# One kernel, one change: more head sums on TensorE, layer normalisation moved to the head of the step, scatters split over two steps

## The reference

```python
x = x + attn(xn) + ffn(xn)
# attn: 8 heads of 16 within each row; no row looks at another
q, k, v = split(xn @ W_qkv.T + b_qkv); each head of q, k, v is divided by its norm
q, k     -> three rounds of mixing neighbouring heads (entangle)
scores   = |einsum('sid,sjd->sij', conj(q), k)|**2 * gain[c]       # 4 circuits c
w        = sqrt(softmax(scores, -1) + 1e-12)
weighted = einsum('sij,sjd->sid', w, v)                            # 4 circuits
out      = sum over c of sup[c] * sign(weighted) * clip(|weighted|, 1e-6, 1), times a phase, @ W_out.T + b_out
# ffn: top-2 of 8 experts per row, gelu(x @ W1[e] + b1[e]) @ W2[e] + b2[e], weighted by a softmax of two
```

## Time and profile before

| | us |
|---|---|
| median of 3 runs | 1745.51 (1744.3 to 1752.1) |
| the profiled execution | 1748.88 |
| its span, first to last instruction | 1747.1 |
| busy: VectorE, TensorE, GpSimd, ScalarE | 1376.4, 1228.0, 889.0, 772.2 |
| mean granted clock of TensorE | 0.837 of 2.4 GHz |

### The profile page before, as it was taken

One profiled execution on the slowest core, in us unless ns is written; L12 is line 12 of the kernel. 1 busy time (PEld: TensorE's weight loads), 2 busy tenths in 40 slices (PEclk: granted clock), 3 DMA queues, 4 the chain that ended last, 5 costly groups with the idle time before them and its releaser, 6 DMA issues.

```text
span 1747.1 us, 19553 instructions
## 1 busy us (share of the span) xinstructions
PE 1228.0 (70%) x6013; PEld 939.7 (54%) x6013; DVE 1376.4 (79%) x1622; ACT 772.2 (44%) x1606; POOL 889.0 (51%) x579
## 2 busy tenths in 40 slices
PE   4576878676787887677877777778677777876221
PEld 2354756555475665555556465656456565655121
DVE  5548888877888888987888898976879798888763
ACT  4344544345454454535435463644345354442110
POOL 1343515476353645477355363667536363536674
PEclk9988988788898888888878898889788898887565
DMA  7242322224223231433314232333213232230101
GB/s 225 69 128 82 91 74 68 84 70 120 70 87 88 69 108 49 122 97 94 91 37 126 62 115 67 93 97 103 87 49 116 67 109 74 87 89 18 31 14 46
DMA packets 110669, 147.24 MB, mean 84 GB/s; under 512 B 14921, under 2 KB 84198, under 8 KB 110054
## 3 DMA queue, kind: packets, MB, share of 16 engines
q1 hardware_dynamic: 101350, 125.01, 23.9%
q0 software_dynamic: 8192, 16.79, 3.1%
q10 hardware_dynamic: 1024, 4.20, 1.9%
HBM read 113.81 MB, written 32.13 MB: 84 GB/s over the span
## 4 chain that ended last, share of the span: by engine, by line
PE 36%; DVE 25%; POOL 15%; issue 15%; ACT 7%; DMA 1%; SPq 0%; ACTq 0%; POOLq 0%; DVEq 0%
POOL prod L1212 11%; PE ps_h L638 6%; PE ps_f L646 5%; PE ps_r L755 5%; PE ps_r L756 4%; DVE u_sgn L1684 3%; PE ps_t L715 3%; DVE prod L1582 3%; DVE u L1610 2%; DVE fxyT L1641 2%; DVE pat L1610 2%; POOL got L1247 2%; PE ps_f L648 2%; PE ps_k L702 2%; PE ps_r L741 2%
## 5 line engine op out<-in xcount | busy, mean ns | idle before, releaser
L1212 POOL TENSOR_TENSOR prod<-expo,vT 128x512 f32<-128x512 f32 x192 | 400.8, 2117 | 463.4 <-ACT expo L1033 313.8
L638 PE MATMUL ps_h<-turned,w_tile 128*128 128x128 f32 x1248 | 216.5, 330 | 179.1 <-ACT turned L1063 178.0
L638 PEld LDWEIGHTS ps_h<-turned,w_tile 128*128 128x128 f32 x1248 | 198.1, 237 | 219.8 <-ACT turned L1063 197.1
L1204 POOL TENSOR_TENSOR prod<-kq 128x1024 f32<-128x1024 f32 x64 | 149.6, 2358 | 199.5 <-ACT kq L1012 144.8
L1070 ACT ACTIVATE hid<-ps_h,w_tile 128x128 f32<-128x128 f32 x624 | 177.4, 367 | 165.3 <-PE ps_h L638 159.7
L1586 DVE TENSOR_TENSOR prod<-expo,vT 128x2048 f32<-128x2048 f32 x80 | 234.7, 2952 | 16.4 <-PE ps_t L715 8.6
L1610 DVE TENSOR_REDUCE u<-prod 128x256 f32<-128x2048 f32 x80 | 182.5, 2281 | 73.4 <-POOL prod L1212 72.8
L1610 DVE TENSOR_REDUCE pat<-prod 128x128 f32<-128x2048 f32 x96 | 218.6, 2279 | 9.7 <-POOL prod L1204 8.0
L646 PE MATMUL ps_f<-w_tile,hid 128*128 128x128 f32 x1248 | 197.8, 311 | 0.3 <-ACT hid L1070 0.2
L715 PE MATMUL ps_t<-prod,ident 128*128 128x256 f32 x768 | 173.7, 383 | 32.6 <-DVE prod L1586 27.1
L646 PEld LDWEIGHTS ps_f<-w_tile,hid 128*128 128x128 f32 x1248 | 186.9, 229 | 1.6 <-issue 0.8
(11 more groups left out here) (257 smaller groups left out, 2155.4 us busy)
## 6 DMA issues: line engine op xcount, KB each, us to landing
w_tile<-w_cat SPq DMA_DIRECT2D x156, 514.0 KB
x_tile<-rows_in SPq DMA_DIRECT2D x156, 64.0 KB, 2.6
rows_out<-turned SPq DMA_DIRECT2D x156, 64.0 KB
rows_in<-u SPq DMA_DIRECT2D x2, 2496.0 KB, 11.6
yacc<-in_L_attn_query_dram SPq DMA_DIRECT2D x16, 256.0 KB, 4.4
out_dram<-yacc SPq DMA_DIRECT2D x16, 256.0 KB, 3.2
x_sb<-in_L_attn_query_dram SPq DMA_DIRECT2D x11, 256.0 KB, 4.6
b_tile<-in_L_ffn_b_dram SPq DMA_DIRECT2D x156, 0.5 KB
```

The costliest lines, as they stand in the source:

```text
L638: last = nc.tensor.matmul(ps_h[:, n % 2, c, :], w_tile[:, n % WS, c * P:(c + 1) * P], turned[:, x_turn(n) % FS, 0, :], start=True, stop=True)
L1204: last = pool.tensor_tensor(set_of(2, part), q, other, ALU.mult)
L1212: last = pool.tensor_tensor(dst[:, at], w[:, at], v[:, at], ALU.mult)
```

## The change

PE_UNITS becomes w0 to w3, all made by VectorE: w0 and w1 are summed in the bank ps_q, w2 and w3 in ps_t. GpSimd makes w4, w5 and w6, all summed by VectorE; VectorE still makes and sums w7. Block j's layer_norm_stats and invert_sd move to the head of VectorE's step, its sd, scaling and transposed copy move up in ScalarE's order (ahead of copy_tile(k, 3) and tiles 5), and turn_x(j) and score(j) move in TensorE's order from the tail to behind grow_once and grow_once_more. q_operands(k, 1) is issued ahead of the step's first expert tile, and q_operands(n, 0) behind the ninth, since its bank ps_q is now in use. Rows of groups 1 and 2 are scattered 10 tiles in steps 2 and 6, and the last 6 in steps 3 and 7, each time behind p5; group 3 is scattered in step 10, 12 tiles behind p5 and 4 behind w6.

```diff
-POOL_UNITS = [("pattern", 2), ("pattern", 5), ("weighted", 1), ("weighted", 4), ("weighted", 6)]
+POOL_UNITS = [("pattern", 2), ("pattern", 5), ("weighted", 4), ("weighted", 5), ("weighted", 6)]
-PE_UNITS = [("weighted", 0), ("weighted", 1), ("weighted", 5)]
+PE_UNITS = [("weighted", m) for m in range(4)]
-FIRST_ROWS = 10
+SCATTERED = {0: ((0, 16),), 1: ((0, 4), (4, 8), (8, 10), (10, 10), (10, 13), (13, 16)),
+             2: ((0, 4), (4, 8), (8, 10), (10, 10), (10, 13), (13, 16)), 3: ((0, 5), (5, 10), (10, 12), (12, 16))}
-        ps_u = ps_t.rearrange("p (m c) -> p m c", m=2)
+        ps_u = [bank.rearrange("p (m c) -> p m c", m=2) for bank in (ps_q, ps_t)]
@@ TensorE @@
                     k_operands(k, 1)
+                if exists(k):
+                    q_operands(k, 1)
                 tiles(k, 0, 1)
-                if exists(k):
-                    q_operands(k, 1)
...
                     grow_once(n)
-                tiles(k, 5, 6)
...
+                if exists(j):
...
                     turn_x(j)
+                tiles(k, 5, 6)
+                if exists(n):
+                    grow_once_more(n)
+                if exists(j):
                     score(j)
...
+                if exists(k):
+                    sums(k, ("weighted", 0))
+                if exists(k):
+                    sums(k, ("weighted", 1))
+                if exists(n):
+                    k_operands(n, 0)
+                if exists(k):
+                    if exists(j):
+                        pe.wait_ge(scores_ready.sem, scores_ready.value(j))
...
+                    sums(k, ("weighted", 2))
                 if exists(far):
                     project(far, [0])
                 tiles(k, 8, 9)
                 if exists(far):
                     project(far, [1])
...
+                if exists(n):
+                    if exists(k):
                         pe.wait_ge(abs_ready.sem, abs_ready.value(k, 1))
-                    sums(k, ("weighted", 5))
+                    q_operands(n, 0)
+                if exists(k):
+                    sums(k, ("weighted", 3))
@@ ScalarE @@
-                    abs_sign(o, 4)
+                    abs_sign(o, 3)
                 if exists(n):
                     norm_sqrt(n)
+                if exists(j):
+                    ln_sd(j)
...
                     copy_mT(o)
+                if exists(j):
+                    layer_norm(j)
                 if exists(k):
                     copy_tile(k, 3)
...
                 tiles(k, 4, 5)
+                if exists(j):
+                    copy_xT(j)
...
                     abs_sign(k, 1)
                     abs_sign(k, 2)
-                    abs_sign(k, 3)
@@ GpSimd @@
+            def scatter_part(k, part):
+                for g, at in ((routed_group(k), part), (routed_group(k - 1) if k >= 0 else None, 4 + part)):
+                    if g is not None and at < len(SCATTERED[g]):
+                        scatter(g, range(*SCATTERED[g][at]))
...
                     products(k, ("pattern", 5))
-                if routed is not None:
-                    scatter(routed, range(0, FIRST_ROWS))
-                if exists(k):
-                    products(k, ("weighted", 1))
+                if exists(n):
+                    scatter_part(k, 0)
+                    scatter_part(k, 1)
+                    scatter_part(k, 2)
+                if exists(k):
                     products(k, ("weighted", 4))
-                if routed is not None:
-                    scatter(routed, range(FIRST_ROWS, GT))
-                if exists(k):
+                    products(k, ("weighted", 5))
                     products(k, ("weighted", 6))
+                    scatter_part(k, 3)
@@ VectorE @@
                     sums(o, ("weighted", 6))
+                if exists(j):
+                    layer_norm_stats(j)
                 if exists(n):
                     norm_squares(n)
...
                     normalise(n)
+                if exists(j):
+                    invert_sd(j)
...
-                if exists(j):
-                    layer_norm_stats(j)
...
-                if exists(j):
-                    invert_sd(j)
...
                 if exists(j):
                     keep_scores(j)
                 if exists(k):
+                    probabilities(k)
+                if exists(k):
+                    products(k, ("weighted", 0))
+                if exists(n):
+                    grown_twice(n, 0)
+                if exists(k):
+                    products(k, ("weighted", 1))
+                if exists(n):
+                    grown_twice(n, 1)
+                if exists(k):
+                    sums(k, ("weighted", 4))
+                if exists(k):
+                    products(k, ("weighted", 2))
+                    products(k, ("weighted", 3))
+                if exists(k):
                     products(k, ("weighted", 7))
+                    sums(k, ("weighted", 5))
                     sums(k, ("weighted", 7))
```

More of the change, by code:

```diff
@@ L714, in sums @@
                 for j in range(NH):
-                    last = nc.tensor.matmul(ps_u[:, ABS_PARTS[part].index(unit[1]), :], ident[:], prod[:, slot, j * 256:(j + 1) * 256],
+                    last = nc.tensor.matmul(ps_u[part][:, ABS_PARTS[part].index(unit[1]), :], ident[:], prod[:, slot, j * 256:(j + 1) * 256],
                                             start=(j == 0), stop=(j == NH - 1))
@@ L823, in _ @@
                     k_operands(k, 1)
-                tiles(k, 0, 1)
                 if exists(k):
                     q_operands(k, 1)
+                tiles(k, 0, 1)
                 if routed is not None:
@@ L857, in _ @@
                     grow_once(n)
+                if exists(j):
+                    if exists(o):
+                        pe.wait_ge(attn_added.sem, attn_added.value(o))
+                    elif exists(k):
+                        pe.wait_ge(scores_ready.sem, scores_ready.value(j - 1))
+                    else:
+                        pe.wait_ge(rank_read.sem, rank_read.value(routed))
+                    turn_x(j)
                 tiles(k, 5, 6)
@@ L860, in _ @@
                     grow_once_more(n)
+                if exists(j):
+                    score(j)
                 tiles(k, 6, 7)
@@ L873, in _ @@
                     k_operands(n, 0)
-                    q_operands(n, 0)
-                if exists(j):
-                    if exists(k):
-                        pe.wait_ge(abs_ready.sem, abs_ready.value(k, 1))
-                    else:
-                        pe.wait_ge(rank_read.sem, rank_read.value(routed))
-                    turn_x(j)
-                    score(j)
+                if exists(k):
+                    if exists(j):
+                        pe.wait_ge(scores_ready.sem, scores_ready.value(j))
+                    else:
+                        pe.wait_ge(attn_added.sem, attn_added.value(o))
+                    sums(k, ("weighted", 2))
                 if exists(far):
@@ L1049, in abs_sign @@
                 if ("weighted", units[0]) in PE_UNITS:
-                    src = ps_u[:, 0:len(units), :].rearrange("p m (c e) -> p (m c) e", c=2)
+                    src = ps_u[n][:, 0:len(units), :].rearrange("p m (c e) -> p (m c) e", c=2)
                 act.activation(u_sgn[:, t, circuits, :], src, ACT.Sign, bias=tiny[:, 0:1]).then_inc(sgn_ready.sem, 1)
@@ L1250, in gather @@
                                                                 axis=0)).then_inc(got_landed.of(at), 16)
+            def scatter_part(k, part):
+                for g, at in ((routed_group(k), part), (routed_group(k - 1) if k >= 0 else None, 4 + part)):
+                    if g is not None and at < len(SCATTERED[g]):
+                        scatter(g, range(*SCATTERED[g][at]))
             for k in STEPS:
-                o, routed = k - 1, routed_group(k)
+                o, n = k - 1, k + 1
                 if exists(k):
@@ L1771, in _ @@
                     value_phase(n)
+                if exists(j):
+                    keep_scores(j)
                 if exists(k):
                     probabilities(k)
-                if exists(j):
-                    invert_sd(j)
                 if exists(k):
@@ L1780, in _ @@
                 if exists(k):
-                    products(k, ("weighted", 2))
+                    products(k, ("weighted", 1))
                 if exists(n):
@@ L1784, in _ @@
                 if exists(k):
-                    sums(k, ("weighted", 2))
+                    sums(k, ("weighted", 4))
+                if exists(k):
+                    products(k, ("weighted", 2))
                     products(k, ("weighted", 3))
-                    products(k, ("weighted", 5))
-                    sums(k, ("weighted", 3))
-                    sums(k, ("weighted", 4))
-                if exists(j):
-                    keep_scores(j)
                 if exists(k):
                     products(k, ("weighted", 7))
+                    sums(k, ("weighted", 5))
```

13 lines of the change are left out of this document (1 added, 12 removed).

## The result

The changed kernel takes 1804.95 us (median of 4 runs, 1801.74 to 1807.9), the kernel before, beside it on the same chip, 1748.8 (4 runs, 1744.3 to 1758.49). The ratio is 1.029, 95% interval 1.025 to 1.034: slower. I had said 1796, in a range of 1740 to 1825. The profiled execution took 1807.9 us, its span is 1806.2, 59.1 more than before. Executions of one kernel differ by up to 1.3% (1740.6 to 1762.3 us in 13 runs of the kernel before in one session), so that a single pair of profiles settles nothing of a few us in the total.

A forecast was written before the change was run, and what follows sets the result against it. VectorE, busy 1376.4 of 1747.1 us, was taken as the bound, each step one chain through it. Terms 31.7 - 1.5 + 7.9 + 5.9 - 17.7 + 17 + 7.5 - 0.5 = +50 gave 1796 us, range 1740 to 1825.

The forecast's parts named there:

- the nine lines of the table: Foretold and measured time changes of nine stretches, prologue to other middles; forecasts from -17.7 to +31.7 us.
- Part 1: VectorE's products in TensorE's layout: 3.89 us against 2.27, four a step instead of two; VectorE's work +0.9 us a step.
- Part 2: Heads: GpSimd's product quarters and VectorE's products of two SBUF operands run in series; p0 2 us later in step 4.
- Rival (a): No series: GpSimd's quarters run beside w0 to w3 as if alone; total -22 us, 1723 us; chance 0.13.
- Part 3: Heads: statistics collide with GpSimd's p2, 5.6 us (bounds 1.6 to 5.6); five heads together +31.7 us.
- Part 4: Scatters: 10.1 us waits for w6 go, -17.7 us; rows of tile 78 late in step 7, +17 us.
- they go: - 17.7: Twelve issues ahead of w6 in steps 2, 6, 10 go: clip -6.9, -3.2, -7.6 us, together -17.7.
- in step 11 the same rows are there in time: Middle of step 11: the scattered rows arrive in time for TensorE; change foretold 0 us.
- Rival (c): Step 7: rows of tile 78 land in time or the work behind has slack; 17 us less, 1779; chance 0.08.
- Rival (d): TensorE does its sums at the lower clock after longer head waits; 2 us more in most steps, 1825; chance 0.08.
- Part 5: Middles of steps 1 to 9: invert_sd, scaling and turn_x on the chain, +7.5 us; prologue -0.5 us.
- Rival (e): The change in the sums does nothing, only the scatters act: -17.7 + 17, no change; chance 0.05.

The follow-up runs named there:

- normalisation alone: Kernel before with only the normalisation moved to the head of the step and q_operands ahead of the first expert tile: ratio 1.018 to the kernel before.
- the scatters as before: Changed kernel with scatters where they were, ten tiles ahead of w4 and six ahead of w6 in the routed step: ratio 1.034 to the kernel before.
- the scatters alone: Kernel before with only the scatters dealt over two steps as in the change: ratio 0.998 to the kernel before.
- one quarter only: Changed kernel in which GpSimd multiplies only the first quarter of w4 and w5, the rest left out: ratio 0.996 to the kernel before.
- group 2 in one step: Changed kernel with group 2's rows all scattered in step 6, 12 tiles ahead of w4, 4 behind w6: ratio 1.023 to the kernel before.
- the sums, 1.055: Kernel before with only the units dealt anew: TensorE sums w0 to w3, GpSimd multiplies w4 to w6: ratio 1.055 to the kernel before.

## Why the prediction was right

The sum held (+ 50 foretold, + 59 in the profiled executions, + 56 between medians), and its main steps are shown, with sizes off in both directions. That the total is so close is in part luck: the nine lines of the table miss by 42 us if one adds the misses without their signs, and by 9 with them.

**Part 1, layout.** Shown: 3.86 and 3.89 in step 4, and 2.29 for the same product in the plain layout, with the same neighbour. The Trainium skill's note on cachelines (SBUF — State Buffer, under "Door 1: The DMA port swizzle") agrees with the direction.

**Part 2, series.** Foretold in step 4: sum w4 at T + 14.0, sum w5 from 31.2, p0 at 35.6. Measured 13.8, 30.4 and 34.9, with waits of 0.82 and 2.38 us (1.3 and 2.5 foretold). Rival (a) asked for w5's sum at T + 26; taking six of eight quarters away brought p0 to 30.8 and the wide products from 4.14 to 3.71 us. The series is shown. The exclusive lock that the Trainium skill describes (SBUF — State Buffer, "Who interferes with whom") is what these rows look like.

**Part 3, statistics beside p2.** Foretold 5.6 us for the statistics, measured 622.64 to 627.94, 5.3. Moving them brought 3.3 in step 4 and 19 us between medians. Clip came at T + 51.1 (52.2 foretold); each of the five heads was foretold 0.9 to 1.3 too long. Heads 0 and 7 were foretold - 1.5 and gave + 3.1: head 0 lies where profiles differ by some us anyway. What I had not seen is how little of these heads belongs to the sums: 3.8 of 5.2 us in step 4 are there with normalisation alone.

**Part 4, scatters.** Both signs right, the sizes not. The step "they go: - 17.7" was 6.5 too good, nearly all of it in step 10 (- 1.4 for - 7.6), and "in step 11 the same rows are there in time" missed 8.9. In step 10 twenty-four issues stand ahead of w4, and I took each at 1.0 + 0.3 us. Two that fall on VectorE's w0 and w1 take 3.56 and 4.69:

```profile
1223.19 0.96 POOL L1243 DMA_INDIRECT rows_in<-xn,row_of  x1 [0.30 <-issue]
1224.45 3.56 POOL L1243 DMA_INDIRECT rows_in<-xn,row_of  x1 [0.31 <-issue]
1228.32 4.69 POOL L1243 DMA_INDIRECT rows_in<-xn,row_of  x1 [0.30 <-issue]
...
1236.83 4.91 POOL L1221 TENSOR_TENSOR prod<-expo,vT 128x512 f32<-128x512 f32 x4
```

```profile
1223.30 3.87 DVE L1601 TENSOR_TENSOR prod<-expo,vT 128x2048 f32<-128x2048 f32 x1 [1.28 <-ACT expo L1043]
...
1228.29 3.88 DVE L1601 TENSOR_TENSOR prod<-expo,vT 128x2048 f32<-128x2048 f32 x1
...
1241.77 2.29 DVE L1625 TENSOR_REDUCE u<-prod 128x256 f32<-128x2048 f32 x1 [4.85 <-POOL prod L1221]
```

w4 begins at T + 14.8 and its sum waits 4.85 us. In step 11 the rows are not quite in time: TensorE waits 4.0 us for x_tile. But it waits 11.9 there in the kernel before, which the prediction doesn't mention, so this wait is not the loss. That has two halves. First, clip takes 5.50 us instead of 1.21, since p2 stands behind eight issues that follow w6 (VectorE, then GpSimd):

```profile
1275.92 5.50 DVE L1696 TENSOR_SCALAR u<-u 128x2048 f32<-128x2048 f32 x1 [0.92 <-ACT u L1063]
```

```profile
1275.70 4.63 POOL L1213 TENSOR_TENSOR prod<-kq 128x1024 f32<-128x1024 f32 x2
```

These 4.3 us are what the run with the scatters as before gives back. The prediction had the series of GpSimd and VectorE, but not that the scatters move p2 onto clip. Second, TensorE. From 1296 to 1316 its granted clock is 0.58 (0.87 in the same stretch of the kernel before, 1254 to 1274), and VectorE waits 5.6 us for grow_once (1.4 before). With the scatters alone it is 0.66 and 3.4, with the scatters as before 0.60 and 5.6, and with one quarter only 0.91 and 1.3. That the low clock stands there is measured. What set it off is not shown by any run here.

```profile
1276.00:1296.00 20.00, 11.75 (x78) 10.32 (x78) 19.86 (x15) 11.46 (x25) 15.05 (x11) 0.91 0.47 141
1296.00:1316.00 20.00, 17.58 (x57) 12.76 (x58) 12.95 (x12) 4.61 (x9) 6.53 (x4) 0.58 0.26 67
```

At tile 78 I foretold 16 us of waiting and a loss of 17; it was 11.6 and 13.5. TensorE reached the tile 6.9 us after the end of p5, where the prediction has 4.7, and the rows were loaded 18.5 us after it, where it has 20.7 (its landing and its load were too slow). Putting group 2 back takes the wait but only 6.4 of the 13.5, mostly since p2 then meets clip. Rival (c) falls. Rival (d), TensorE at the lower clock, is seen in step 11, with some 2 us in step 7, and not in all steps; what it costs was read from waits beside it and not tested.

**Part 5.** + 7.5 foretold for the middles, + 12.9 measured, the largest in steps 1, 3, 8 and 9 (3.1, 5.5, 2.7 and 3.7), with steps 10, 12 and 14 shorter; the prologue gave 5.6 where I had 0.5. How much of these is the change and how much the difference between two profiles stays open. Rival (e) had one half right: the scatters alone change nothing (0.998).

## What to carry to other kernels

A queue's issues are work: put the ones that nobody awaits behind the product that somebody does, and look what the next product behind them then falls on (here clip or the normalisation, 4 to 6 us each). Twelve descriptor issues moved behind one product gave 1.6%; the new deal of products, sums and normalisation lost 2.9%. Before two engines that share the memory's path are given more work at once, multiply out their instructions in series; a second engine's share of such work was nearly free here only beside sums and beside work from PSUM. When a part of a change looks bad alone (the sums, 1.055), look whether another part exists to make room for it before you sum them.

## What the runs showed of the hardware that was not expected

An indirect DMA's issue on GpSimd, mostly 0.96 us, took 3.56 and 4.69 us when it fell on VectorE's product of two SBUF operands; the next in the row was back at 0.96. In another kernel (group 2 in one step) the same two places show 3.60 and 4.70. By these two places it is held as a quarter of a product is: both end 0.84 us after VectorE's product.

TensorE reading fp32 columns 32 bytes apart took 639 ns for 256 columns against 384 to 388 adjoining ones, at a higher mean clock.

A VectorE instruction of four elements a partition, 0.16 us where nothing stands beside it, took 5.84 us where four quarters of a GpSimd product ran back to back (5.83 in the run of the scatters alone): it is held not by one neighbour but by a row of them.

VectorE's clip has one SBUF operand and two constants. It took 5.50 and 5.94 us instead of 1.22 where it met GpSimd's p2: not only products of two SBUF operands are held.
